# Attention heads of an AdaLN block: a one-piece row gather, key loads with another dimension outermost, and inverse roots in Newton steps

## The chip, the cores and the metric

The kernel runs on one core of a Trainium2 chip. Its time is the device time in microseconds (us), as the median of several runs. The core has a matrix engine (TensorE, PE in the profile), a vector engine (VectorE, DVE), a scalar engine (ScalarE, ACT), a general engine (GpSimd, POOL), and a queue engine (SyncE, SP) that here only starts transfers. They run in parallel and wait for each other through semaphores.

## The reference

x is (2, 2048, 256): two batches of 2048 tokens. Each batch goes through an attention layer that computes only the rows it selects, and then through a soft mixture of experts.

```
h = layernorm(x) * (1 + ca) + sa
q, k, v = heads of h @ Wq + bq, h @ Wk + bk, h @ Wv + bv      # 16 heads of width 16
scores = q k^T / 4
top_idx = top_k(scores.max(-1) - scores.mean(-1), 307)        # 307 of 2048 queries in each head
out = zeros; out[top_idx] = softmax(q[top_idx] k^T / 4) v
x = x + ga * (out @ Wo + bo)
h = layernorm(x) * (1 + cb) + sb
xn = h / max(norm(h), 1e-12) * 16 * gamma                     # per token
logits = xn sn^T                                              # 8 experts x 128 slots
eo = experts(softmax over tokens); y = softmax over slots of logits, times eo
x = x + gb * y
```

## The kernel before, in words

Tokens lie in 16 tiles of 128. For each batch in turn there are a search (score maxima of all 16 heads), a selection (a rank for each query in each head), and the attention over the selected queries, here "the head loop". The expert layers of both batches come after that: logits of 16 tiles, 8 experts, and a mix of 16 tiles. Queries and keys are kept in DRAM as three bfloat16 parts, whose products, six of them for each of the 16 dimensions (96 rows), restore float32 precision.

The head loop is the stage that the change touches most. The order on each engine is written out by hand. For head n, PE does this (`pe_head`, with line numbers of the kernel before):

- `scores` (L1960), in pairs k = 0 to 7, two products each: keys of 2 x 128 tokens against the 307 selected queries. ScalarE takes each pair out of PSUM with an exponential (`exps`, L905). The pairs use two PSUM places in turn, so pair k waits for the exponential of pair k-2. Pairs 0 and 1 of head n+1 are done inside head n, after its pair 7.
- `values` (L1969): 2 x 8 tiles of values times exponentials. The first half stands behind pair 5. The second half stands behind pairs 0 and 1 of the next head, and waits for all eight exponentials of its own head.
- `gather` (L1941): 16 products of a one-hot matrix, one for each token tile, which pick the 307 query rows. VectorE builds the one-hot matrix (`onehot`, L1414). The result goes to ScalarE (`take_gathered`, L893), then PE copies its parts to the 96 rows (`spread`, L1948, with a constant matrix `spread_rows`), and ScalarE takes that (`take_queries`, L898) as the queries of the next head. Gather and spread use one PSUM bank.
- `rows` (L1977) and `turn` (L1984): the row numbers of the selected queries, and the transposition of the finished output of the head before. VectorE divides (`finish`). In batch 1, GpSimd then scatters the rows to DRAM with three indirect transfers for each head (L726). In batch 0 those scatters are put off to the search of batch 1.

SP loads the 96 key rows (4 KB each) of a head in three transfers, of 48, 32 and 16 rows (`head_keys`, L487). There are two key buffers, so the transfers of head n+2 start when pair 7 of head n is through, and pair 0 of head n+2 waits for them. In `k_parts` the 48 rows are 3 parts x 16 dimensions.

The other part of the change is the square roots. In batch 1's head loop the second layer norm and the row norms of batch 0 are made on the side: variances in `spread`, a ScalarE square root (`root`, L946), a correction on VectorE (`refine`, L1102 to L1110), the normalised tile (`second_norm`, L1318 and L1322), its square on ScalarE (`square`, L952), another root for `rms`, and `xn_tile` (L1337), which gives the expert stage its input. The square root and the exponential live in different tables of ScalarE. For batch 1 the same is done at the start of, and inside, the mix of batch 0's experts (L2165 transpositions, L2175 products, L1027 and L1020 on ScalarE).

Of the kernel before, what the change touches and what calls it, by code (L numbers as in the profile page):

```python
# [17 lines left out]
I32 = mybir.dt.int32  # L18
# [6 lines left out]
LN_EPS = 1e-5  # L25
# [50 lines left out]
def adaln_block(nc, x, Wq, bq, Wk, bk, Wv, bv, Wo, bo, gamma, slot_gamma, slot_embeds,  # L76
# [60 lines left out]
    with ExitStack() as ctx:  # L137
# [241 lines left out]
        def _(sp):  # L379
# [102 lines left out]
            def head_keys(b, i, par):  # L482
# [124 lines left out]
        def _(pool):  # L607
# [31 lines left out]
            for half in range(2):  # L639
                for at, part in enumerate((0, 0, 0, 1, 1, 2)):  # L640
                    cols = spread_rows[:, at * DH:(at + 1) * DH]
                    g.affine_select(out=cols, in_=cols, compare_op=ALU.not_equal, fill=1.0, base=-(half * HALF_ROWS + part * DH), pattern=[[-1, DH]], channel_multiplier=1)
# [159 lines left out]
        def _(act):  # L802
# [85 lines left out]
            def attend(b):  # L888
# [53 lines left out]

            def root(n):

                act.wait_ge(var_ready, n)
                s.activation(rs_y[:], rs_v[:], ACT.Sqrt).then_inc(sqrt_done, 1)  # L946
# [7 lines left out]
            def experts(b):  # L954
# [78 lines left out]
                if b == 0:  # L1033
                    root(7)
                    for t in range(NT - 2):
# [4 lines left out]
                        if t == NT // 2:  # L1040
                            root(8)
                else:
                    with act.Fori(0, NT // 2 - 1) as i:
                        for par in range(2):
                            combine_turned(i, par)
                            combine_exp(i, par, par + 2)
# [48 lines left out]
        def _(dve):  # L1095
# [16 lines left out]


# [186 lines left out]
            def spread(b):  # L1300
# [7 lines left out]
                v.tensor_scalar(rs_v[:], mv[:, :, 1], LN_EPS, None, ALU.add).then_inc(var_ready, 1)  # L1308

            def spread_roots(b):  # L1310

                dve.wait_ge(sqrt_done, 4 + 3 * b)
                refine(NT, rstd[:], 1.0)
# [11 lines left out]
            def row_spread(b, at, end):  # L1325

                dve.wait_ge(ss_ready, 1 + NT * b + end)
                v.tensor_scalar(rs_v[:, at:end], ss[:, at:end], NORM_MIN * NORM_MIN, None, ALU.max).then_inc(var_ready, 1)

            def row_roots(n, at, end):  # L1330

                dve.wait_ge(sqrt_done, n)
                refine(end, rms[:, at:end], RMS, at)
# [72 lines left out]
            def attend(b):  # L1406
# [847 lines left out]
```

## Time and profile before

| | |
|---|---|
| time, median of 3 runs | 1620.09 us (1619.43 to 1622.69) |
| the profiled execution, its own time | 1618.59 us |
| its span in the profile | 1616.8 us |
| PE busy | 1475.0 us (91%) |
| DVE busy | 1201.0 us (74%) |
| ACT busy | 1052.9 us (65%) |
| score products of the head loop, L1960 and L905 | 512 PE products, 256 exponentials |

The profile is of one execution. Its span leaves out 1.8 us of that execution's time. Busy PE time counts overlapping ends, so a PE that is 91% busy still has gaps that matter. What sets the end is read from the chain of waits and from the order in time on each engine. The head loops lie at about 450 to 575 us (batch 0) and 938 to 1071 us (batch 1).

### The profile page before, as it was taken

To read this page: it belongs to the slowest core of one execution; us is meant where nothing else is said; L and a number is where in the kernel's file an instruction comes from. 1 tells how busy PE (TensorE), PEld (TensorE's weight loads), DVE (VectorE), ACT (ScalarE), POOL (GpSimd) and SP (SyncE) were. 2 spreads that over 40 slices of the span, in tenths; PEclk is the share of its full clock that TensorE was granted. 3 is DMA by queue.
4 is the path that set the end of the run, shared out by engine and by line. 5 is a ranking of instruction groups with operands and counts; after the bars stand their busy time and mean duration, and the time that the engine had idled before them with its cause. 6 is when DMAs were issued, how large, how long until landed. Compare 5 with 4: busy or idle time off the path is not lost.

```text
span 1616.8 us, 28401 instructions
## 1 busy us (share of the span) xinstructions
PE 1475.0 (91%) x8701; PEld 806.6 (50%) x8706; DVE 1201.0 (74%) x2750; ACT 1052.9 (65%) x1436; POOL 271.3 (17%) x334
## 2 busy tenths in 40 slices
PE   7999999998889989999998888979999999989999
PEld 3532222223434422222223634434899886489988
DVE  6679999999876669999999877756765443675511
ACT  4578888887677778888886557753433572334464
POOL 2440000003510051111111213330111000011100
PEclk9999999999999999999999989999999999999999
DMA  5861111121522201111212211120144202014410
GB/s 173 258 164 39 39 49 49 39 86 46 163 80 70 66 21 44 40 41 40 52 51 70 78 31 52 52 81 0 40 160 147 89 33 71 0 54 142 161 49 32
DMA packets 93458, 119.39 MB, mean 74 GB/s; under 512 B 22862, under 2 KB 78766, under 8 KB 92860
## 3 DMA queue, kind: packets, MB, share of 16 engines
q1 hardware_dynamic: 90300, 117.66, 23.8%
q0 software_dynamic: 3072, 0.66, 0.3%
q8 instruction: 44, 0.72, 0.2%
q14 instruction: 42, 0.34, 0.1%
HBM read 93.46 MB, written 24.79 MB: 73 GB/s over the span
## 4 chain that ended last, share of the span: by engine, by line
PE 46%; DVE 32%; issue 13%; ACT 4%; DMA 3%; POOL 1%; SPq 0%; DVEq 0%; another core or an unknown queue 0%; ACTq 0%; PEld 0%; PEldq 0%; POOLq 0%
DVE work_area L1282 25%; PE psum L2111 7%; PE psum L2175 6%; PE psum L1969 4%; PE psum L1960 4%; PE psum L2054 4%; PE psum L2122 3%; DVE big_area L1282 2%; PE psum L2131 2%; PE psum L1941 2%; DMA work_area<-heads_out 2%; PE psum L1769 2%; PE psum L2165 2%; PE psum L1794 1%; ACT big_area L962 1%
## 5 line engine op out<-in xcount | busy, mean ns | idle before, releaser
L1282 DVE CUSTOM_DVE_ANT_0 work_area<-psum,work_area 128x1024 f32<-128x1024 f32 x512 | 589.1, 1220 | 8.0 <-PE psum L1830 4.3
L883 ACT ACTIVATE work_area<-psum 128x1024 f32<-128x1024 f32 x512 | 510.4, 1027 | 74.5 <-DVE big_area L1282 30.7
L1830 PE MATMUL psum<-work_area 96*128 96x512 bf16 x1024 | 309.2, 384 | 47.9 <-DVE big_area L1282 6.8
L1820 PE MATMUL psum<-work_area 96*128 96x512 bf16 x1024 | 305.4, 380 | 7.4 <-ACT work_area L883 1.7
L1830 PEld LDWEIGHTS psum<-work_area 96*128 96x128 bf16 x1024 | 63.4, 97 | 266.3 <-DVE big_area L1282 243.5
L1820 PEld LDWEIGHTS psum<-work_area 96*128 96x128 bf16 x1024 | 88.8, 98 | 153.0 <-ACT work_area L883 58.3
L905 ACT ACTIVATE work_area<-psum 128x614 f32<-128x614 f32 x160 | 102.3, 682 | 39.0 <-PE psum L1960 38.4
L2111 PE MATMUL psum<-work_area,xn 128*128 128x128 f32 x1024 | 117.7, 276 | 0.0
L2175 PE MATMUL psum<-expert_out,work_area 128*128 128x256 f32 x512 | 115.6, 379 | 1.1 <-ACT work_area L1027 1.1
L2054 PE MATMUL psum<-slots_T,work_area 128*128 128x512 f32 x256 | 116.5, 599 | 0.0
L2111 PEld LDWEIGHTS psum<-work_area,xn 128*128 128x128 f32 x1024 | 116.3, 193 | 0.2
L1414 DVE TENSOR_SCALAR big_area<-iota,rank 128x308 bf16<-128x308 f16 x512 | 113.8, 300 | 0.1
L1960 PE MATMUL psum<-work_area 99*128 99x307 bf16 x512 | 94.4, 303 | 20.0 <-issue 6.6
L2175 PEld LDWEIGHTS psum<-expert_out,work_area 128*128 128x128 f32 x512 | 95.1, 190 | 13.1 <-ACT work_area L1027 1.3
L962 ACT ACTIVATE big_area<-psum 128x1024 f32 (+1 forms) x32 | 32.8, 1024 | 88.5 <-PE psum L2054 88.5
L1619 DVE SCALAR_TENSOR_TENSOR work_area<-psum,rz,x_res 128x256 f32<-128x256 f32 x32 | 15.5, 484 | 100.0 <-PE psum L2175 65.5
L741 POOL DMA_INDIRECT heads_out<-Wqk_sb x48 | 48.7, 1015 | 213.8 <-DVE big_area L1282 213.0
L1504 DVE TENSOR_TENSOR work_area<-work_area,big_area 128x1024 f32<-128x1024 f32 x32 | 39.2, 1226 | 49.1 <-ACT big_area L962 49.1
L757 POOL TENSOR_TENSOR work_area<-big_area,work_area 128x1024 f32 (+1 forms) x16 | 38.6, 2415 | 196.8 <-PE psum L2115 172.6
L1960 PEld LDWEIGHTS psum<-work_area 99*128 99x128 bf16 x512 | 39.9, 100 | 62.2 <-ACT work_area L905 20.2
L2054 PEld LDWEIGHTS psum<-slots_T,work_area 128*128 128x128 f32 x256 | 46.8, 193 | 47.6 <-issue 47.2
L905 ACT ACTIVATE expert_out<-psum 128x614 f32<-128x614 f32 x96 | 62.5, 680 | 9.8 <-PE psum L1960 8.2
(262 smaller groups left out, 2085.4 us busy)
## 6 DMA issues: line engine op xcount, KB each, us to landing
work_area<-in_L_ffn_w_dram SPq DMA_DIRECT2D x32, 1024.0 KB, 5.2
work_area<-k_parts SPq DMA_DIRECT2D x192, 64.2 KB
work_area<-q_parts SPq DMA_DIRECT2D x192, 64.0 KB
k_parts<-work_area SPq DMA_DIRECT2D x24, 384.0 KB, 3.5
q_parts<-work_area SPq DMA_DIRECT2D x16, 384.0 KB, 3.1
big_area<-q_parts SPq DMA_DIRECT2D x16, 384.0 KB, 5.9
work_area<-k_parts SPq DMA_DIRECT2D x32, 192.0 KB
x_res<-in_L_attn_x_dram SPq DMA_DIRECT2D x8, 512.0 KB, 6.4
```

What stands on the lines that cost most here:

```text
L883: s.activation(SC[:, t % 4], PS[:, 2 * (n % 2):2 * (n % 2) + 2].rearrange("p a n -> p (a n)"), ACT.Relu).then_inc(relu_done, 1)
L905: s.activation(PX[k][:, :, 0:U], PS[:, 2 * (k % 2):2 * (k % 2) + 2, 0:U], ACT.Exp, scale=SCALE).then_inc(p_ready, 1)
L962: s.activation(row(LS, i * 2 + par), PS[:, 2 + 2 * par:4 + 2 * par].rearrange("p a n -> p (a n)"), ACT.Identity).then_inc(lg_copied, 1)
L1282: v.tensor_tensor_reduce(SC[:, t % 4], PS[:, 4 + 2 * (t % 2):6 + 2 * (t % 2)].rearrange("p a n -> p (a n)"), SC[:, t % 4], 1.0, -3.0e38, A ...
L1414: last = v.tensor_scalar(OH[:, par, t], iota[:], rank[:, t, bass.ds(h, 1)], None, ALU.is_equal)
L1820: last = mm(PS[:, 2 * (n % 2) + k], QS1[par][0:TERMS, t * P:(t + 1) * P], KS[par][0:TERMS, k * 512:(k + 1) * 512], start=True, stop=True)
L1830: last = mm(PS[:, 4 + 2 * (t % 2) + k], QS1[par][0:TERMS, t * P:(t + 1) * P], KS[par][0:TERMS, K1 + k * 512:K1 + (k + 1) * 512], start=Tru ...
L1960: last = mm(PS[:, 2 * (k % 2) + kk, 0:U], K2S[n % 2][0:TERMS + 3, kt * P:(kt + 1) * P], QS[0:TERMS + 3, n % 2, 0:U], start=True, stop=True)
L1969: last = mm(PS[at:at + DH + 1, 6 - n % 2, 0:U], V[:, kt, i * 2 + n], PX[kt // 2][:, kt % 2, 0:U], start=(kt < 4), stop=(kt >= NT - 4), ski ...
L2054: last = mm(PS[:, 2 + 2 * par + k], XT[:, par, cc], SNT[:, cc, k * 512:(k + 1) * 512], start=(cc == 0), stop=(cc == DC - 1))
L2111: last = mm(PS[:, cc, 0:P], XN[:, t, cc * P:(cc + 1) * P], E1[:, t], start=(t == 0), stop=(t == NT - 1))
L2175: last = mm(PS[:, 5 - par, 0:D], E2T[:, par, e], EO[:, e], start=(e == 0), stop=(e == E - 1))
```

## The change

There are three edits.

1. `pe_head`: head n+1's gather is done whole (16 products) behind pairs 2 and 3 of head n. Before, tiles 8 to 15 stood there, and tiles 0 to 7 of head n+2's gather stood behind pairs 6 and 7.
2. `head_keys`: the DRAM side of each key transfer is given with the dimension ahead of the part, so its outermost size is 16 and not 3, 2 or 1. Each transfer still moves the same rows. Since the rows arrive in another order, `spread_rows` is filled to match.
3. The inverse roots of the second layer norm and of the row norms come from `inverse_roots` on VectorE: a first guess from the bits and three Newton steps, ten small instructions. `root` is gone from ScalarE. `spread_roots` moves from behind head 2 to behind head 1. The row norms of tiles 0 to 7 stand behind head 13, and the first two `xn_tile` behind head 14. The mix loop of the last batch on ScalarE is written out.

```diff
-                    sp.dma_start(K2S[par][at:at + n * DH, :], k_parts[b][0:n, bass.ds(h0, DH), K1:KW]).then_inc(k2_in[par], 16)
+                    sp.dma_start(K2S[par][at:at + n * DH, :], k_parts[b][0:n, bass.ds(h0, DH), K1:KW].rearrange("r p n -> p r n")).then_inc(k2_in[par], 16)
...
                 for h in range(H):
                     act_head(h // 2, h % 2, h < H - 1)
                     if b == 1:
-                        if h == 1:
-                            root(4)
                         if h < H - 1:
                             for t in tiles_of_head(h - 1):
                                 square(0, t)
                 if b == 1:
-                    root(5)
                     for t in range(NT - 4, NT):
                         square(0, t)
-                    root(6)
...
+            def inverse_roots(out_, at, end):
+
+                v_, y_, a_ = rs_v[:, at:end], rs_y[:, at:end], rs_a[:, at:end]
+                v.tensor_scalar(y_.bitcast(I32), v_.bitcast(I32), -0.5, float(0x5F3759DF), ALU.mult, ALU.add).then_inc(vstep, 1)
+                dve.wait_ge(vstep, vs.next())
+                for k in range(3):
+                    v.tensor_tensor(a_, y_, y_, ALU.mult).then_inc(vstep, 1)
+                    dve.wait_ge(vstep, vs.next())
+                    v.scalar_tensor_tensor(out=a_, in0=a_, scalar=-0.5, in1=v_, op0=ALU.mult, op1=ALU.mult).then_inc(vstep, 1)
+                    dve.wait_ge(vstep, vs.next())
+                    v.scalar_tensor_tensor(out=out_ if k == 2 else y_, in0=a_, scalar=1.5, in1=y_, op0=ALU.add, op1=ALU.mult).then_inc(vstep, 1)
+                    dve.wait_ge(vstep, vs.next())
...
-                        if h == 2:
-                            spread_roots(0)
-                        if h == H - 1:
-                            row_spread(0, 0, NT - 4)
+                        if h == 1:
+                            spread_roots()
+                        if h == H - 3:
+                            row_norms(0, 0, NT // 2)
+                        if h == H - 2:
+                            for par in range(2):
+                                xn_tile(0, par, par)
                         second_norm(0, tiles_of_head(h))
                     finish(PAIRS - 1, 1, 1)
-                    row_roots(5, 0, NT - 4)
-                    for par in range(2):
-                        xn_tile(0, par, par)
-                    row_spread(0, NT - 4, NT)
-                    row_roots(6, NT - 4, NT)
+                    row_norms(0, NT // 2, NT)
...
                     if later > 0 and not first:
-                        gather(i, n + 1, range(0 if second else NT // 2, NT))
+                        gather(i, n + 1, range(NT))
...
-                    if later > 1 and not first:
-                        gather(i, n + 2, range(NT // 2))
                     if not first:
                         turn(i, n - 1)
```

The first place is on PE, one head of the loop, from the spread for the next head to pairs 4 and 5 of the next head. `work_area` and `expert_out` hold queries, keys and exponentials, `big_area` the one-hot matrix or the values. Before:

```order
L1948 MATMUL psum<-work_area,spread_rows 101x307
L1960 MATMUL psum<-work_area 128x307 x4
L1941 MATMUL psum<-big_area,work_area 64x307 x8
L1984 MATMUL psum<-identF,work_area 128x128 x3
L1960 MATMUL psum<-work_area 128x307 x4
L1969 MATMUL psum<-expert_out,big_area 17x307 x4
L1969 MATMUL psum<-work_area,big_area 17x307 x4
L1960 MATMUL psum<-work_area 128x307 x4
L1941 MATMUL psum<-big_area,work_area 64x307 x8
L1977 MATMUL psum<-idx_rows,work_area 128x1 x2
L1977 MATMUL psum<-idx_rows,work_area 51x1
L1960 MATMUL psum<-work_area 128x307 x4
```

The same place on PE after the change, where the lines of these functions have moved up by three:

```order
L1945 MATMUL psum<-work_area,spread_rows 101x307
L1957 MATMUL psum<-work_area 128x307 x4
L1981 MATMUL psum<-identF,work_area 128x128 x3
L1957 MATMUL psum<-work_area 128x307 x4
L1966 MATMUL psum<-expert_out,big_area 17x307 x4
L1966 MATMUL psum<-work_area,big_area 17x307 x4
L1957 MATMUL psum<-work_area 128x307 x4
L1938 MATMUL psum<-big_area,work_area 64x307 x16
L1974 MATMUL psum<-idx_rows,work_area 128x1 x2
L1974 MATMUL psum<-idx_rows,work_area 51x1
L1957 MATMUL psum<-work_area 128x307 x4
```

Eight gather products went from between pairs 6, 7 and the transposition to behind pairs 2, 3. Between pairs 6, 7 and the next pairs 0, 1 only the three transpositions are left.

The second place is on DVE, at the start of the mix of batch 0's experts: the last rows before the first `second_norm` of batch 1 (`mean_var` is the variances, `rstd` the inverse roots). Before:

```order
L1305 BN_AGGR mean_var<-stat 128x2 x16
L1308 TENSOR_SCALAR rs_v<-mean_var 128x16
L1555 TENSOR_TENSOR work_area<-psum,work_area 128x256
L1557 TENSOR_TENSOR expert_out<-work_area,mod_rows_sb 128x256
L1102 RECIPROCAL rs_a<-rs_y 128x16
L1104 TENSOR_TENSOR rs_a<-rs_a,rs_v 128x16
L1106 TENSOR_TENSOR rs_a<-rs_a,rs_y 128x16
L1108 RECIPROCAL rs_a<-rs_a 128x16
L1110 TENSOR_SCALAR rstd<-rs_a 128x16
L1318 SCALAR_TENSOR_TENSOR xn<-x_res,mean_var,mod_rows_sb 128x256 x2
```

After the change, on DVE, from the same expert output to the same step:

```order
L1555 TENSOR_TENSOR expert_out<-work_area,mod_rows_sb 128x256
L1313 TENSOR_SCALAR rs_v<-mean_var 128x16
L1106 TENSOR_SCALAR rs_y<-rs_v 128x16
L1109 TENSOR_TENSOR rs_a<-rs_y 128x16
L1111 SCALAR_TENSOR_TENSOR rs_a<-rs_a,rs_v 128x16
L1113 SCALAR_TENSOR_TENSOR rs_y<-rs_a,rs_y 128x16
L1109 TENSOR_TENSOR rs_a<-rs_y 128x16
L1111 SCALAR_TENSOR_TENSOR rs_a<-rs_a,rs_v 128x16
L1113 SCALAR_TENSOR_TENSOR rs_y<-rs_a,rs_y 128x16
L1109 TENSOR_TENSOR rs_a<-rs_y 128x16
L1111 SCALAR_TENSOR_TENSOR rs_a<-rs_a,rs_v 128x16
L1113 SCALAR_TENSOR_TENSOR rstd<-rs_a,rs_y 128x16
```

Between the expert output and the first `second_norm` there stood five small instructions, and now there are eleven.

The third place is on ACT, at the end of batch 1's head loop. Before, the last exponentials are followed by a table load and two roots:

```order
L905 ACTIVATE work_area<-psum 128x2x307 x2
L946 ACT_TABLE_LOAD
L946 ACTIVATE rs_y<-rs_v 128x16
L952 ACTIVATE work_area,sumsq<-xn 128x256 x4
L946 ACTIVATE rs_y<-rs_v 128x16
L958 ACTIVATE work_area<-psum 128x256
```

After the change, on ACT, L958 has become L951:

```order
L907 ACTIVATE work_area<-psum 128x2x307 x3
L907 ACTIVATE expert_out<-psum 128x2x307 x3
L907 ACTIVATE work_area<-psum 128x2x307 x2
L945 ACTIVATE work_area,sumsq<-xn 128x256 x4
L951 ACTIVATE work_area<-psum 128x256
```

Both roots and the table load are gone, and the four squares lead straight to the first copy of the expert stage.

## Rows read from the trace of the kernel before

**Rows 1.** PE in time, one head of batch 0; us start, us length, [idle before].

```profile
528.80 0.69 PE L1960 MATMUL psum<-work_area 99*128 99x307 bf16 x4
529.58 0.71 PE L1941 MATMUL psum<-big_area,work_area 128*64 128x307 bf16 x8
530.22 0.55 PE L1984 MATMUL psum<-identF,work_area 128*128 128x128 f32 x3
531.33 0.68 PE L1960 MATMUL psum<-work_area 99*128 99x307 bf16 x4 [0.56 <-issue]
531.94 0.71 PE L1969 MATMUL psum<-expert_out,big_area 128*17 128x307 f32 x8
533.11 0.70 PE L1960 MATMUL psum<-work_area 99*128 99x307 bf16 x4
536.59 0.69 PE L1960 MATMUL psum<-work_area 99*128 99x307 bf16 x4
```

**Rows 2.** SP in time, the key transfers issued two heads earlier.

```profile
522.10 1.88 SPq L487 DMA_DIRECT2D work_area<-k_parts  x3
```

**Rows 3.** ACT in time, in that head.

```profile
529.33 1.25 ACT L905 ACTIVATE work_area<-psum 128x614 f32<-128x614 f32 x2
531.79 1.26 ACT L905 ACTIVATE work_area<-psum 128x614 f32<-128x614 f32 x2 [1.21 <-PE psum L1960]
```

**Rows 4.** The chain of waits in the last heads of batch 0.

```profile
562.08 7.15 DMA work_area<-k_parts
```

**Rows 5.** Stretches: busy time (count) by engine, PE clock, DMA share, GB/s.

```profile
562.00:569.00 7.00, 5.65 (x60) 2.67 (x59) 1.89 (x8) 5.45 (x10) 0.00 (x0) 1.00 0.21 57
570.10:573.50 3.40, 3.30 (x23) 1.24 (x16) 0.48 (x1) 1.68 (x4) 0.00 (x0) 0.50 0.02 5
```

**Rows 6.** The page's DMA issues: count, KB each, us from issue to landing.

```profile
k_parts<-work_area SPq DMA_DIRECT2D x24, 384.0 KB, 3.5
big_area<-q_parts SPq DMA_DIRECT2D x16, 384.0 KB, 5.9
```

**Rows 7.** PE in time: a whole gather, first and last spread of 13 periods, last head.

```profile
464.73 1.24 PE L1941 MATMUL psum<-big_area,work_area 128*64 128x307 bf16 x16
467.94 0.34 PE L1948 MATMUL psum<-work_area,spread_rows 128*101 128x307 bf16 x1
566.46 0.34 PE L1948 MATMUL psum<-work_area,spread_rows 128*101 128x307 bf16 x1
569.94 0.63 PE L1969 MATMUL psum<-expert_out,big_area 128*17 128x307 f32 x4
```

**Rows 8.** PE in time, batch 1: the wait in head 2, and spreads of 12 periods.

```profile
959.43 1.01 PE L1960 MATMUL psum<-work_area 99*128 99x307 bf16 x4 [1.70 <-ACT work_area L905]
963.05 0.34 PE L1948 MATMUL psum<-work_area,spread_rows 128*101 128x307 bf16 x1
1010.79 0.34 PE L1948 MATMUL psum<-work_area,spread_rows 128*101 128x307 bf16 x1
1059.26 0.34 PE L1948 MATMUL psum<-work_area,spread_rows 128*101 128x307 bf16 x1
```

**Rows 9.** POOL in time, the third scatter of one head of batch 1.

```profile
1010.14 1.07 POOL L726 DMA_INDIRECT heads_out<-work_area  x1 [0.30 <-issue]
```

**Rows 10.** ACT in time, that head, and the end of batch 1's head loop.

```profile
1012.02 0.43 ACT L898 ACTIVATE work_area<-psum 101x307 bf16<-101x307 f32 x1 [0.93 <-PE psum L1948]
...
1073.16 0.19 ACT L952 ACTIVATION_READ_ACCUMULATOR work_area<-xn 128x1 f32 x1
1075.38 0.37 ACT L958 ACTIVATE work_area<-psum 128x256 f32<-128x256 f32 x1
```

**Rows 11.** DVE in time, the third tile's input, and a small step of `refine`.

```profile
1078.24 0.48 DVE L1337 SCALAR_TENSOR_TENSOR work_area<-xn,rms,gamma_row 128x256 f32<-128x256 f32 x1 [1.75 <-POOL xn L751]
...
1284.99 0.17 DVE L1106 TENSOR_TENSOR rs_a<-rs_a,rs_y 128x16 f32<-128x16 f32 x1
```

**Rows 12.** PE in time, the second tile of the first mix.

```profile
1289.08 3.29 PE L2175 MATMUL psum<-expert_out,work_area 128*128 128x256 f32 x14 [1.09 <-ACT work_area L1027]
```

More of the change, by code:

```diff
@@ L639, in _ @@
             for half in range(2):
-                for at, part in enumerate((0, 0, 0, 1, 1, 2)):
-                    cols = spread_rows[:, at * DH:(at + 1) * DH]
-                    g.affine_select(out=cols, in_=cols, compare_op=ALU.not_equal, fill=1.0, base=-(half * HALF_ROWS + part * DH), pattern=[[-1, DH]], channel_multiplier=1)
+                at = 0
+                for part, n in enumerate((3, 2, 1)):
+                    cols = spread_rows[:, at:at + n * DH].rearrange("p (d r) -> p d r", r=n)
+                    g.affine_select(out=cols, in_=cols, compare_op=ALU.not_equal, fill=1.0, base=-(half * HALF_ROWS + part * DH), pattern=[[-1, DH], [0, n]], channel_multiplier=1)
+                    at += n * DH
                 cols = spread_rows[:, TERMS:TERMS + 5]
@@ L941, in take_heads @@
                 s.activation(AT[:, t % 2], PS[:, turn_bank(b, t), turn_at(b, t):turn_at(b, t) + D], ACT.Identity).then_inc(at_ready, 1)
-            def root(n):
-                act.wait_ge(var_ready, n)
-                s.activation(rs_y[:], rs_v[:], ACT.Sqrt).then_inc(sqrt_done, 1)
             def square(b, t):
@@ L1033, in experts @@
                 if b == 0:
-                    root(7)
                     for t in range(NT - 2):
@@ L1039, in experts @@
                             square(1, k)
-                        if t == NT // 2:
-                            root(8)
-                else:
-                    with act.Fori(0, NT // 2 - 1) as i:
-                        for par in range(2):
-                            combine_turned(i, par)
-                            combine_exp(i, par, par + 2)
+                else:
+                    for t in range(NT - 2):
+                        combine_turned(t // 2, t % 2)
+                        combine_exp(t // 2, t % 2, t % 2 + 2)
                 for par in range(2):
@@ L1307, in spread, with spread_roots @@
                 dve.wait_ge(vstep, vs.next())
[L1308 to L1313, printed above, removed]
+            def spread_roots():
+                v.tensor_scalar(rs_v[:], mv[:, :, 1], LN_EPS, None, ALU.add).then_inc(vstep, 1)
+                dve.wait_ge(vstep, vs.next())
+                inverse_roots(rstd[:], 0, NT)
             def second_norm(b, tiles):
@@ L1323, in second_norm, with row_norms @@
                                            op0=ALU.mult, op1=ALU.add).then_inc(h2_ready, 1)
-            def row_spread(b, at, end):
+            def row_norms(b, at, end):
                 dve.wait_ge(ss_ready, 1 + NT * b + end)
[L1328 to L1333, printed above, removed]
+                v.tensor_scalar(rs_v[:, at:end], ss[:, at:end], NORM_MIN * NORM_MIN, 1.0 / D, ALU.max, ALU.mult).then_inc(vstep, 1)
+                dve.wait_ge(vstep, vs.next())
+                inverse_roots(rms[:, at:end], at, end)
             def xn_tile(i, par, n):
@@ L1594, in experts @@
                     expert_out(E - 1, 0, vs.next())
-                    spread_roots(1)
+                    spread_roots()
                 else:
@@ L1627, in experts @@
                             v.memset(CM, -3.0e38).then_inc(cmax_done, 1)
-                            row_spread(1, 0, NT)
-                            row_roots(8, 0, NT)
+                            row_norms(1, 0, NT)
                         if t >= NT - 2:
```

1 line of the change is left out of this document (removed).

## The prediction

> **What bounds the kernel now.** I read the chain of waits first, to see which stages carry the end; then PE, ACT and SP in order of time inside one head of the loop; then stretches of time, for the transfers and PE's clock; last the page's table of transfers. In the head loop PE is the bound, with one gap in each head: 0.56 us ahead of pairs 0 and 1 of the next head [rows 1]. The view can't name its releaser ("issue"). I read it as the key transfers. Those for the pair at 531.33 were started at 522.10 [rows 2], so if they end the gap they take 9.2 us from first issue to landing. Where the chain does name them, in the last head of batch 0, it shows 7.15 us of DMA behind the last issue at 562.08, till 569.23 [rows 4]. With the 1.88 us that the three issues take, that is 9.0 us, the same length. In that stretch 0.21 of the 16 DMA engines is busy, at 57 GB/s [rows 5]: a head's keys (96 rows of 4 KB, 393 KB) need 6.9 us at that rate. So few engines do the work, and it is their time that each head waits for.
>
> Call T the start of pairs 6 and 7 of a head. T is 528.80, and the next is 536.59: a period of 7.79. Over 13 periods of batch 0 it is (566.46 - 467.94) / 13 = 7.58 [rows 7]. The loop closes on the keys: they start at T + 1.1 (522.10, where T was 528.80 - 7.79 = 521.01), and land 9.1 later, which must be before pair 0 of two heads on.
>
> **The change part by part.**
>
> *The key transfers.* The nearest rows for another shape are transfers of the same 384 KB on 128 rows: 3.5 us from issue to landing for a write, 5.9 for a load [rows 6]. With 1.9 of issues the new length is between 1.9 + 3.5 = 5.4 and, if nothing changes, 9.1. I take 5.4 to 6, since the load of 5.9 is of short runs and this is of 4 KB rows. The wait is then not late in any head: pair 0 comes at T + period + 1.3, so the transfers have 7.5 us. What is late next is ScalarE, below.
>
> The Trainium skill ("DMA: Bandwidth & Descriptors", section on why a DMA increments its semaphore by 16 and not by 1) says that such a transfer is split over k engines, k being the largest number up to 16 that divides the outermost size of both sides. By it, the three transfers ran on 3, 2 and 16 engines, and now run on 16 each. The trace agrees with the first half: a share of 0.21 is 3.4 engines [rows 5]. No row shows the second half. By the rule the time on the busiest engine falls from 33 rows of 4 KB to 6; by the rows alone it may not fall at all, and that is the rival that ends slower.
>
> *The gather.* Products neither come nor go, eight of them move. They were the work that PE had between pairs 6, 7 and the next pairs 0, 1, and that covered ScalarE: exponentials 6 and 7 run from 529.33 to 530.58, that is to T + 1.78 [rows 3]. Before, PE reached the next pair 0 at T + 2.53 with the wait, and at about T + 1.8 without. Now only the transposition stands between, so PE is there at about T + 1.0 and waits: pair 0 for exponential 6, pair 1 for exponential 7. Its signal arrives 0.06 after the end (533.05 to 533.11) [rows 1, 3], so pair 1 starts at T + 1.84, takes 0.31 (half of 531.33 to 531.94), and the value products start at T + 2.17, where they started at T + 3.14. From there to the next T it was 536.59 - 531.94 = 4.65. Eight more gather products stand in it now: a whole gather takes 1.24 and a half 0.71, so 0.53 more [rows 1, 7]. New period: 2.17 + 4.65 + 0.53 = 7.35. So of the gap that the transfers leave, some is handed back as a wait on ScalarE. With the old order the period without the gap would be 7.79 - 0.56 = 7.23 or less: the move alone costs some 0.1 to 0.3 a head. Behind the gather, `take_gathered` on ScalarE comes 0.53 later; exponential 4 waits for pair 4, which is 0.53 later itself, so this costs nothing. On VectorE the one-hot of a head is ready half a head earlier than it is needed.
>
> Batch 0: 98.5 - 13 x 7.35 = 2.9 us. Its last head: the value products stood at 569.94, and come at 566.46 + 0.17 + 2.17 = 568.80, so 1.1. Behind the long wait PE ran at half clock (1.2 GHz; granted 0.50) from 570.10 for 3.4 us, and did in it what takes 1.7 at the full 2.4 GHz [rows 5]. Without a long wait ahead of it I don't expect the fall, and take 1.2 of the 1.7, as ScalarE bounds a head with no gather (0 to 1.7).
>
> Batch 1: 12 periods take 1059.26 - 963.05 = 96.2, so 8.02 each [rows 8]. Here the signals of PE's products come late around GpSimd's scatters: the spread starts at 1010.79, and ScalarE gets it 1.23 later, idle for 0.93, while GpSimd runs an indirect transfer from 1010.14 to 1011.21 [rows 8 to 10]. That delay stands in the period before (gather and pair 0 wait behind it). Whether it stays exposed depends on where the scatters fall in the new order. They start after `finish`, which follows the transposition. That stands some 0.3 earlier against the value products, and the pairs 4, 5 and the spread stand 0.53 later, so by my count they fall mostly outside. The ends are 7.35 (no delay) and 7.92 (one exponential of 0.57 late in each head). I take 7.5: 96.2 - 90 = 6.2 (1.2 to 8.0). The last head of batch 1 gains 1.1 as that of batch 0.
>
> *The roots.* Removed from ScalarE in head 2: PE waited 1.70 there behind two table loads [rows 8]. On VectorE the eleven small instructions of about 0.21 each (0.17 [rows 11] and an estimate of 0.04 between them) take 2.3 us behind head 1, where VectorE waits over 2 us a head; that is 1.7 gained. The row norms behind head 13 lie where no one-hot is built any more, and are hidden too. At the end of the loop the first expert tiles are ready before, so the first copy of the expert stage starts when ScalarE has done its squares: at 1073.35 where it was 1075.38 [rows 10], 2.0, and 0.1 for a small instruction gone ahead of them. The third tile isn't late by this: its input came at 1078.24 behind GpSimd's copy [rows 11], and the first tile's logits hold PE till then anyway. At the mix the chain is the other way: VectorE now does eleven instructions instead of five between the expert output and `second_norm` (one of the six more had been hidden), ScalarE's square and copy wait for it, and PE already waited 1.09 for that copy [rows 12]. So 6 x 0.21 = 1.2 less what the removed table loads give ScalarE: I take a loss of 1.1 (0 to 1.3). The roots inside the mix are hidden before and after; so are the table loads in the last mix, where PE has work for a whole tile.
>
> The sum: 2.9 + 1.1 + 1.2 + 6.2 + 1.1 + 1.7 + 2.1 - 1.1 = 15.2 us off the profiled execution's 1618.6, which gives 1603.4. That execution lies 1.5 below the median of the runs, so the forecast for the median is 1605.
>
> **The rivals.**
>
> *A. The scatters' delay stays in every head of batch 1.* For it: it stood in nearly every head before, and the moved gather's own signal may now fall into it. Against it: by count the exponentials 6 and 7 start clear of it. Then 7.92 in batch 1, 1.2 instead of 6.2: 5 us less, 1610.
>
> *B. The transfers stay as slow.* This ends slower, as the filler is gone and the wait isn't. With a length of 9.1 and a start at T + 1.1, pair 0 must stand at T + 10.2, and it comes at T + period + 1.26. With g as the gap, 7.35 + g + 1.26 + g = 10.2 gives g = 0.8 and a period of 8.15. Batch 0 loses 13 x 0.57 = 7.4, batch 1 some 12 x 0.2 = 2.4, and the rest gives 1.2 + 1.7 + 2.1 - 1.1 = 3.9: 5.9 slower, 1626. It decides from a length of about 8 us (7.35 + g = 7.58, g = 0.23) on. Against it: the same kilobytes on 128 rows land in 3.5 to 5.9.
>
> *C. More than the count.* The delays in batch 1 vanish, the clock's fall at the head of the expert stage too (PE is idle there for 2 us less), and the heads run at 7.25. Then 13 x 0.1 + 12 x 0.25 = 4.3 from the periods, and some 1.5 from the clock on top: 1599.
>
> *D. Almost nothing.* The move of the gather costs what the transfers give (a period of 7.6 in batch 0, 8.0 in batch 1), and only the ends stay: 1.1 + 1.2 + 1.1 + 1.7 + 2.1 - 1.1, 6 us: 1614.
>
> **How the numbers follow.** My forecast 0.52, A 0.18, C 0.16, D 0.08, B 0.06. The range for 8 in 10 is 1598 to 1612.5, from C to past A. A measurement of this kernel tells 0.2% (3.2 us) from no change. Faster by more than that are the forecast, A, C and most of D: 0.91. Same: 0.04, from D and B. Slower: 0.05, B.
>
> **What would show it.** Period of the spread, batch 0, at 7.3 to 7.4, with PE's two short waits now ahead of pairs 0 and 1 and released by the exponentials; 7.06 to 7.2 would show that ScalarE isn't late, 7.6 and more that the gather's move or the transfers cost. The key transfers landing within 6 us of their first issue, spread over more engines. No wait for keys in the last heads, and no half clock at 570. In batch 1 a period of 7.5. No table load in head 2. The first expert copy right behind the squares, and a longer wait of PE for its second tile at the first mix. The forecast is wrong if the key transfers are late again, or if batch 1's heads stay at 8.

## The result, and where the time went

The changed kernel takes 1617.67 us (median of 18 runs, 1614.1 to 1621.43), the kernel before 1620.32 beside it (18 runs, 1616.37 to 1625.61). The ratio is 0.9983, 95% interval 0.9976 to 0.999: by 0.2%, no change that counts. 1605.0 was forecast, within 1598 to 1612.5. The forecast was wrong.

The profiled execution has a span of 1619.5 us (own time 1621.43), so it is on the slow side of its runs by 3.8, and 2.7 above the span shown of before. The page of after:

```profile
span 1619.5 us, 28340 instructions
PE 1481.0 (91%) x8701; PEld 810.5 (50%) x8706; DVE 1204.9 (74%) x2775; ACT 1033.8 (64%) x1418; POOL 271.0 (17%) x328
```

**Batch 0 came as forecast.** PE in one head of batch 0, after (start, duration, line, products; the last bracket is PE's wait and its releaser). It answers to [rows 1]:

```profile
519.97 0.69 PE L1957 MATMUL psum<-work_area 99*128 99x307 bf16 x4
520.49 0.49 PE L1981 MATMUL psum<-identF,work_area 128*128 128x128 f32 x3
521.31 0.92 PE L1957 MATMUL psum<-work_area 99*128 99x307 bf16 x4 [0.33 <-ACT work_area L907]
522.16 0.71 PE L1966 MATMUL psum<-expert_out,big_area 128*17 128x307 f32 x8
523.95 1.24 PE L1938 MATMUL psum<-big_area,work_area 128*64 128x307 bf16 x16
527.33 0.69 PE L1957 MATMUL psum<-work_area 99*128 99x307 bf16 x4
```

T is 519.97, the next 527.33: a period of 7.36. The wait ahead of pair 0 has a name now, exponential 6 on ScalarE, and the value products start at T + 2.19 (2.17 forecast). The keys are early:

```profile
520.78 1.83 SPq L487 DMA_DIRECT2D work_area<-k_parts  x3
```

By the trace's semaphore records the last piece of these three transfers landed at 524.87, 4.1 us after the first issue. For the transfers issued at 522.10 before [rows 2], it was 531.24, so 9.1 us, 0.09 before pair 0 at 531.33 [rows 1].

**Batch 1 did not.** The spreads of batch 1 in after, and those of batch 0 (first and last start of a line's instructions):

```profile
L1945 PE MATMUL psum<-work_area,spread_rows x13: 335/335/335, 958.5 to 1062.0; 128*101 128x307 bf16 x13
L1945 PE MATMUL psum<-work_area,spread_rows x14: 335/335/335, 468.2 to 564.0; 128*101 128x307 bf16 x14
```

12 periods take 103.5 us, 8.62 each, where before took 96.2 [rows 8] and 90 was forecast. What waited, after, 958 to 1062 us (who, for what: us in total, times, longest):

```profile
ACT work_area L895 <- remote: 20.9, 10, 2.4
PE psum L1945 <- ACT work_area L895: 4.1, 10, 0.7
PE psum L1957 <- ACT work_area L907: 2.8, 12, 0.3
PE psum L1957 <- ACT expert_out L907: 2.4, 10, 0.2
```

L895 is `take_gathered`, which waits for the gather's last product and waited 0.6 us in all in the same stretch of before. In the head at 1023 us that product ends at about 1024.7 by the timeline, its increment (the signal) is recorded at 1026.64, and `take_gathered` starts at 1026.66. The signals of `rows` and of pairs 4 and 5, whose products end between 1025.0 and 1025.6, are recorded from 1026.69 to 1026.78. The last of the head's three scatters ran from 1024.97 to 1026.06. Behind `take_gathered`, ScalarE's queue holds exponentials 4 and 5, `take_queries` and exponentials 6 and 7. Exponential 4 starts at 1026.99; it couldn't have started before 1026.73 in any case, as its own signal was late too.

PE's clock fell besides. It was at 1.2 GHz three times inside these 12 periods (at 969.9, 1004.0 and 1055.2 us, 3.4 us each), and never inside those of before. One of the three, with the stretches around it (PE, PEld, DVE, ACT, POOL busy, granted clock, DMA share, GB/s):

```profile
961.00:969.90 8.90, 7.54 (x73) 3.48 (x73) 6.48 (x29) 5.75 (x13) 3.08 (x3) 1.00 0.20 49
969.90:973.30 3.40, 3.40 (x22) 0.93 (x20) 0.50 (x3) 1.41 (x5) 1.96 (x3) 0.50 0.41 118
973.30:977.00 3.70, 3.70 (x43) 1.95 (x42) 3.67 (x17) 2.78 (x5) 1.06 (x1) 1.00 0.04 6
```

The three periods with a fall are 9.5, and the one behind it is 7.8. The first of the 12 is 8.69, and the six others are 8.43 in the mean. So the late signals make 8.43 of 7.36. The three falls add 0.4, 0.5 and 1.1 us (each with the shorter period behind it, which the last doesn't have in the count).

### The profile page after: what moved, and what is told of

It reads as the page before. It is cut to its first block, busy times and chain, and to the rows that moved or that the text cites. A ratio compares the mean times of both kernels' runs of the same rounds, so it can differ in the third digit from the quotient of the medians.

```text
span 1619.5 us, 28340 instructions
## 1 busy us (share of the span) xinstructions
PE 1481.0 (91%) x8701; PEld 810.5 (50%) x8706; DVE 1204.9 (74%) x2775; ACT 1033.8 (64%) x1418; POOL 271.0 (17%) x328
## 4 chain that ended last, share of the span: by engine, by line
PE 45%; DVE 32%; issue 13%; ACT 6%; DMA 3%; POOL 1%; SPq 0%; DVEq 0%; ACTq 0%
DVE work_area L1284 25%; PE psum L2106 7%; PE psum L2170 6%; PE psum L1966 5%; PE psum L2049 4%; PE psum L1957 4%; PE psum L2117 3%; DVE big_area L1284 2%; PE psum L1938 2%; PE psum L2126 2%; ACT work_area L907 2%; PE psum L1766 2%; DMA work_area<-heads_out 2%; PE psum L2160 2%; PE psum L1791 1%
## 5 line engine op out<-in xcount | busy, mean ns | idle before, releaser
L1957 PE MATMUL psum<-work_area 99*128 99x307 bf16 x512 | 100.4, 306 | 19.2 <-ACT work_area L907 10.1
L728 POOL DMA_INDIRECT heads_out<-work_area x48 | 50.2, 1046 | 102.8 <-DVE work_area L1441 91.3
```

Source lines behind the costliest of these rows:

```text
L728: g.indirect_dma_start(out=heads_out[b], out_offset=bass.IndirectOffsetOnAxis(ap=IDX[0:w, par, j:j + 1], axis=0), in_=ON[0:w, par, j], in_ ...
L1957: last = mm(PS[:, 2 * (k % 2) + kk, 0:U], K2S[n % 2][0:TERMS + 3, kt * P:(kt + 1) * P], QS[0:TERMS + 3, n % 2, 0:U], start=True, stop=True)
```

## The experiments

The runs came to six chips or more, and these are of two kinds. I call them by their trace: on chips with **late signals** increments of PE's semaphores are recorded up to 2.2 us after the product beside scatters, and ScalarE starts only then; on the **others** none is late. Periods are from one profile each; b0 is 13 periods of batch 0, b1 the last 12 of batch 1; the last column is the ratio to the kernel before on the same chip.

| kernel | chip | b0 | b1 | median us | before | ratio (95%) |
|---|---|---|---|---|---|---|
| before (first profile) | late | 7.58 | 8.02 | 1620.32 | | |
| after | late | 7.36 | 8.62 | 1617.67 | 1620.32 | 0.9983 (0.9976-0.999) |
| keys_only | late | 7.06 | 7.78 | 1606.43 | 1618.99 | 0.9921 (0.9903-0.994) |
| gather_only | late | 8.02 | 8.50 | 1628.10 | 1618.99 | 1.0046 (1.0029-1.0063) |
| roots_only | late | 7.64 | 7.98 | 1617.48 | 1618.99 | 0.9994 (0.9978-1.0009) |
| keys_roots | late | 7.06 | 7.92 | 1603.76 | 1618.99 | 0.9901 (0.9883-0.9919) |
| halves_in_b1 | other | 7.36 | 7.15 | 1599.49 | 1613.17 | 0.9915 (0.9895-0.9935) |
| deferred_one | other | 7.36 | 7.36 | 1620.00 | 1613.17 | 1.0035 (1.0019-1.0051) |
| deferred | other | 7.06 | 7.13 | 1613.11 | 1613.17 | 0.9998 (0.9982-1.0014) |
| copies_on_act | other | 7.06 | 7.15 | 1593.44 | 1613.17 | 0.9883 (0.9863-0.9904) |
| after_again | other | 7.36 | 7.36 | 1602.70 | 1614.92 | 0.9925 (0.9905-0.9944) |
| before_again | other | 7.69 | 7.94 | 1614.05 | 1614.92 | 0.9989 (0.9975-1.0003) |
| keys_roots_again | other | 7.06 | 7.15 | 1595.99 | 1614.92 | 0.9881 (0.986-0.9901) |
| no_scatter | other | 7.36 | 7.36 | 1601.35 | 1614.92 | 0.9922 (0.9902-0.9942) |
| after_third | other | 7.36 | 7.36 | 1600.84 | 1616.05 | 0.9907 (0.9875-0.9939) |
| no_scatter_third | other | 7.36 | 7.36 | 1601.86 | 1616.05 | 0.9910 (0.988-0.994) |
| copies_on_act_third | other | 7.06 | 7.15 | 1592.84 | 1616.05 | 0.9856 (0.9824-0.9888) |
| half_scatters | other | 7.36 | 7.36 | 1600.91 | 1613.93 | 0.9914 (0.988-0.9948) |
| half_scatters_2 | late | 7.36 | 7.36, then 8.43 | 1610.06 | 1621.20 | 0.9928 (0.990-0.9956) |

### One part of the change at a time

keys_only is the kernel before with this edit (and `spread_rows` filled to match):

```diff
-  k_parts[b][0:n, bass.ds(h0, DH), K1:KW]).then_inc(k2_in[par], 16)
+  k_parts[b][0:n, bass.ds(h0, DH), K1:KW].rearrange("r p n -> p r n")).then_inc(k2_in[par], 16)
```

> The kernel before with the key transfers in the new order of rows, nothing else of the change. Theory S (GpSimd's scatters hold back TensorE's signals, and the gather in one piece puts its own signal in that window): without the moved gather batch 1 keeps the period of before or a little less, 7.8 to 8.0 us; batch 0 loses the wait for keys: 7.1 to 7.25 instead of 7.58, so 13 x 0.4 = 5 off; no 7 us wait in the last head. In all 6 to 8 us faster (ratio 0.995 to 0.9965), more than the whole change. Rival T (the new transfers themselves disturb batch 1, by more engines at once): a period of 8.4 in batch 1 as with the whole change, and no gain in all. Rival U (ScalarE bounds the heads in any order): 7.36 in batch 0 here too.

gather_only is the kernel before with `gather(i, n + 1, range(NT))` behind pairs 2 and 3 and without the half behind pairs 6 and 7.

> The kernel before with the gather in one piece behind the second score pair, nothing else. Theory S: batch 1 at 8.4 us a head (8.02 before), 12 x 0.4 = 5 more, with take_gathered on ScalarE waiting some 2 us in each head; batch 0 at about 8.1 since the keys still take 9 us and the filler ahead of pair 0 is gone: 13 x 0.5 = 6.5 more. In all 9 to 13 us slower (ratio 1.006 to 1.008). Rival T (the transfers disturb batch 1, the gather doesn't): batch 1 stays at 8.0 to 8.2, in all 6 to 8 slower.

roots_only has `inverse_roots` and its places, and nothing else. keys_roots is the changed kernel with the gather as before:

```diff
-                        gather(i, n + 1, range(NT))
+                        gather(i, n + 1, range(0 if second else NT // 2, NT))
...
+                    if later > 1 and not first:
+                        gather(i, n + 2, range(NT // 2))
```

> The kernel before with the roots by Newton steps on VectorE, nothing else. Theory S: batch 1's third head 1.4 us shorter, the other heads at 8.02 as before; what the end of the loop gains is mostly given back behind GpSimd's copy of the third tile, and the first mix loses about 1: in all 1 to 3 us faster (ratio 0.998 to 0.9995). Rival V (VectorE's new work is what lengthens batch 1's heads): a period of 8.4 in batch 1 and 2 to 4 us slower in all.

> The changed kernel with the gather in two halves as before: all of the change but the moved gather. Theory S: batch 0 at 7.1 to 7.25, batch 1 at 7.8 to 8.0, the third head without table loads: 8 to 10 us faster than before (ratio 0.994 to 0.995), and so faster than the whole change by 6. Rivals T and V (transfers or roots lengthen batch 1): batch 1 at 8.4 also here and no faster than the whole change (ratio 0.998).

The keys alone give 12.6 us, most of the gain and more than I had expected (6 to 8): 6.7 in batch 0, 2.9 in batch 1's 12 periods. With the roots it is 15.2, where 8 to 10 was expected. The roots alone give 1.5, which the noise doesn't tell from nothing. The gather alone loses 7.5 by the ratio (9 to 13 expected); its profile has the clock at half for 3.4 us in one head of each batch, which took 10.05 and 10.29. So one edit of the three works against the change: keys_roots is 13 us (by the ratios) faster than the whole change on the same kind of chip. T, U and V fall: in keys_only batch 1 is at 7.78 and batch 0 at 7.06, in gather_only batch 1 is at 8.50, and in roots_only at 7.98.

### The gather in one piece, and the scatters

halves_in_b1 keeps the piece in batch 0 and has the two halves in batch 1.

> The changed kernel with the gather of batch 1 in two halves as before; in batch 0 it stays in one piece. Theory S (the piece costs 0.3 us a head by ScalarE's wait in batch 0, and 0.7 to 0.8 in batch 1 where its signal falls into GpSimd's scatters): batch 0 at 7.36, batch 1 at 7.8 to 8.0, in all 1608 to 1610. Rival W (what the piece costs in batch 1 is the same 0.3 as in batch 0, and the rest was the clock, which fell three times in that profile): 1613 to 1614, with batch 1 at 8.1 to 8.2 where no half clock stands.

It ran at 7.06 in all of batch 1's last 11 heads (the mean of 7.15 holds one of 8.11), with the scatters in place: neither S nor W allowed that. The same code in batch 1 had taken 7.92 in keys_roots. The chip was the difference, and the next three runs, all on one chip, ask that question.

> The changed kernel once more, beside the kernel before and two others on one chip, since the runs so far came from two chips whose traces differ: on one, batch 1's heads take 7.8 to 7.9 with halves, TensorE's signals 0.5 to 2.4 us late beside the scatters; on the other the same order takes 7.06 and no signal is late. Theory Y (whether the scatters hold back signals is a property of the chip or of the run, and only where they do does the moved gather cost 11 us in batch 1): where signals are late, a period of 8.4 to 8.6 and 1617 to 1620; where they aren't, 7.36 in both batches, 1602 to 1606 with the kernel before at 1613. Rival Z (the gather in one piece is what brings the late signals, on any chip): 8.4 to 8.6 on either chip.

> The kernel before once more, for its profile on this chip. Theory Y: where signals are late, 7.58 and 8.02 a head in the two batches as in the first profile; where they aren't, 7.5 in both, some 6 us less in all. Its ratio to itself is 1.

> The changed kernel with the gather in two halves. Theory Y: 7.06 in batch 0 on any chip; in batch 1 7.8 to 7.9 where signals are late and 7.06 to 7.15 where they aren't; 1603 or 1594 to 1596. In both cases faster than the whole change: by 13 to 15 us where signals are late, by 26 x 0.3 = 8 where not.

Y holds and Z falls. In after_again the changed kernel has 7.36 in each head of both batches; 13 spreads of batch 1:

```profile
L1945 PE MATMUL psum<-work_area,spread_rows x13: 335/335/335, 953.8 to 1042.2; 128*101 128x307 bf16 x13
```

No signal is late in it, and `take_gathered` waits 2.1 us in all 12 heads where it had waited 20.9 in ten (958 to 1062 us):

```profile
PE psum L1957 <- ACT work_area L907: 4.3, 13, 0.4
ACT work_area L895 <- PE psum L1938: 2.1, 12, 0.2
```

There the change is worth 12.2 and, in after_third, 15.2 us (15.2 forecast). The kernel before is faster on such a chip too, by some 3 to 8 us in the medians, though batch 1 is at 7.94 for 8.02 in the profile. That mean holds one head of 11.92, in which PE waited 1.9 us for the keys and then ran at half clock for 6.8; the eleven others take 7.57. Its keys are late on either kind.

Whether the scatters are the cause can only be seen on a chip with late signals. no_scatter leaves out batch 1's scatters, and ran on two of the others.

> The changed kernel without the scatters of batch 1 (its heads' outputs are computed but not written, so this work is left out). Theory S: where signals are late with the scatters, this kernel's batch 1 has a period of 7.36, that of batch 0, and no late signal: 13 x 1.2 = 14 to 16 less than the changed kernel beside it. Where they aren't late, 7.36 in both and no difference in the heads. Rival W (something else in batch 1's heads): 8 or more stays without the scatters.

> The changed kernel as the reference of this chip. If signals are late here: 8.4 a head in batch 1 where TensorE's clock doesn't fall, 1617 to 1620. If not: 7.36 and 1601 to 1605.

> The changed kernel without the scatters of batch 1 (left out: its heads' outputs are not written). If the scatters hold the signals back: 7.36 a head on any chip, and on one with late signals 13 to 16 us less than the changed kernel. Rival (such a chip delays signals whatever GpSimd does): 8.4 here too.

Where no signal is late, leaving the scatters out changes nothing: 7.36 and 7.36, 1601.35 beside 1602.7, 1601.86 beside 1600.84. The next kernel carries its own control, heads 0 to 7 of batch 1 without scatters and 8 to 15 with:

```diff
-                with pool.Fori(0, PAIRS) as i:
+                with pool.Fori(PAIRS // 2, PAIRS) as i:
                     for par in range(2):
                         scatter(i, par)
```

> The changed kernel, with the scatters of batch 1's heads 0 to 7 left out (those heads are not written) and those of heads 8 to 15 kept. If the scatters hold the signals back, on a chip with late signals: heads 0 to 7 at 7.36, and 8.4 and late signals from head 9 on. If such a chip delays signals by itself: 8.4 in all heads. On a chip without late signals: 7.36 throughout, which decides nothing.

> The changed kernel, with the scatters of batch 1's heads 0 to 7 left out (those heads are not written) and those of heads 8 to 15 kept, once more. If the scatters hold the signals back, on a chip with late signals: heads 0 to 7 at 7.36, and 8.4 and late signals from head 9 on. If such a chip delays signals by itself: 8.4 in all heads. On a chip without late signals: 7.36 throughout, which decides nothing.

half_scatters ran on a chip without late signals (7.36 throughout), half_scatters_2 on one with. Its spreads from 962 to 1001 us, without scatters, and from 1020 to 1050, with them:

```profile
L1945 PE MATMUL psum<-work_area,spread_rows x6: 335/335/335, 963.9 to 1000.7; 128*101 128x307 bf16 x6
L1945 PE MATMUL psum<-work_area,spread_rows x4: 334/335/335, 1024.3 to 1049.6; 128*101 128x307 bf16 x4
```

(1000.7 - 963.9) / 5 = 7.36 and (1049.6 - 1024.3) / 3 = 8.43, in one execution and at full clock. The gather and `take_gathered` in one head of each kind, PE and ScalarE of half_scatters_2, first without scatters:

```profile
997.48 1.24 PE L1938 MATMUL psum<-big_area,work_area 128*64 128x307 bf16 x16
...
1000.69 0.34 PE L1945 MATMUL psum<-work_area,spread_rows 128*101 128x307 bf16 x1
...
998.76 0.43 ACT L895 ACTIVATE work_area<-psum 128x307 bf16<-128x307 f32 x1 [0.18 <-PE psum L1938]
999.37 1.25 ACT L907 ACTIVATE expert_out<-psum 128x614 f32<-128x614 f32 x2 [0.18 <-PE psum L1957]
```

and with them (PE, ScalarE, GpSimd):

```profile
1020.61 1.24 PE L1938 MATMUL psum<-big_area,work_area 128*64 128x307 bf16 x16
...
1024.29 0.34 PE L1945 MATMUL psum<-work_area,spread_rows 128*101 128x307 bf16 x1 [0.41 <-ACT work_area L895]
...
1023.81 0.43 ACT L895 ACTIVATE work_area<-psum 128x307 bf16<-128x307 f32 x1 [2.10 <-remote]
1024.13 1.25 ACT L907 ACTIVATE expert_out<-psum 128x614 f32<-128x614 f32 x2
...
1019.41 0.98 POOL L728 DMA_INDIRECT heads_out<-work_area  x1 [4.61 <-DVE work_area L1441]
1020.70 1.12 POOL L728 DMA_INDIRECT heads_out<-work_area  x1 [0.30 <-issue]
1022.12 1.11 POOL L728 DMA_INDIRECT heads_out<-work_area  x1 [0.30 <-issue]
```

From the gather's start to `take_gathered` it is 1.28 us without scatters and 3.20 with. In this one execution the gather's signal is 0.02 us late in all of the heads without scatters from 954 to 1007 us, and 1.91 to 1.96 in the five with them. The scatters are the cause, on the chips where there are late signals. Whether the products' results land late or only their signals, the trace doesn't tell. In halves (keys_roots) the window hits another signal: the half gather's is on time (0.02 in the last ten heads) and `take_gathered` doesn't wait, but the spread's is late, by 0.74 to 1.06 in twelve heads. This costs 7.92 against 7.15, or 0.77 a head, where the piece pays 1.07.

### The scatters out of the heads

deferred keeps all heads' outputs of batch 1 (as batch 0 does), scatters them during batch 0's logits, and moves GpSimd's copies there to ScalarE; deferred_one has the gather in one piece besides. The core of it:

```diff
+            def scatter_in_logits():
+                pool.wait_ge(on_ready, B * H)
+                for h in range(H):
+                    for j in range(CH):
+                        w = min(P, U - j * P)
+                        g.indirect_dma_start(
+                            out=heads_out[1], out_offset=bass.IndirectOffsetOnAxis(ap=IDX0[0:w, h, j:j + 1], axis=0),
+                            in_=ON0[0:w, h, j], in_offset=None).then_inc(scattered[h % 2], 16)
```

> The changed kernel (gather in one piece) with the scatters of batch 1 moved out of the heads: VectorE keeps all heads' outputs and indices, as in batch 0, GpSimd scatters them while the logits are made, and ScalarE makes the copies that GpSimd made there. Theory S: batch 1's period falls to that of batch 0, 7.36, with no wait of take_gathered on ScalarE beyond 0.3; 13 x 1.1 = 14 us off the changed kernel, 1601 to 1604, if the scatters disturb the logits little. Rival W (the clock, or the work that only batch 1's heads have: the norms on VectorE, the squares on ScalarE): a period of 8 or more stays.

> The changed kernel with the gather in two halves as before and the scatters of batch 1 moved out of the heads as in deferred_one. Theory S: 7.06 in both batches; 12 x 0.85 = 10 us less than with halves and scatters in the heads (1603.8), so 1592 to 1595, and 1590 if the third tile of the expert stage was held up by GpSimd's copy. Rival X (the delay only moves: 48 scatters in 65 us hold back the signals of the logits, or the first transfers of the heads' rows come late): 1600 or more.

X holds: deferred is 17 us behind keys_roots on a like chip (1613.1, 1596.0), where it was expected ahead, and deferred_one 17 to 19 behind after. The chain of waits of deferred (start, duration) and the two rows of PE after it:

```profile
1121.15 0.99 POOL heads_out L753
1122.44 0.96 POOL heads_out L753
1123.71 2.30 DMA heads_out<-Wqk_sb
1126.47 2.44 DMA work_area<-heads_out
```

```profile
1107.83 3.17 PE L2065 MATMUL psum<-slots_T,work_area 128*128 128x512 f32 x7
1128.21 1.43 PE L1868 MATMUL psum<-identF,work_area 128*128 128x128 f32 x4 [17.22 <-issue]
```

GpSimd starts the last of the 48 scatters at 1123.7, it lands 2.3 us later, and the heads' rows can be loaded only then. PE waits 17.2 us, and its clock is at half from 1114.8 for 17.1 us. Neither version ran on a chip with late signals, where the saving in the heads would stand against this; that stays open.

### A version that beats both

copies_on_act is keys_roots with `s.activation(row(XN, i * 2 + n), XS[:, par], ACT.Identity)` behind the copy of each turned tile, in place of GpSimd's copy (batch 0's expert stage alone).

> The changed kernel with the gather in two halves as before, and the copies of the normalised tiles in batch 0's logits on ScalarE instead of GpSimd; the scatters stay in the heads. If the third tile of the expert stage is held up by GpSimd, which still has the last heads' scatters ahead of its copy (theory: that is where the 2.1 us forecast for the start of the expert stage went), the second logits start 1.5 to 2.5 us earlier against the last take_out, and the time is 1602 against 1603.8. If it isn't the copy, no change or some 0.3 a tile of ScalarE's work in the way: 1604.

> Halves, new key transfers, Newton roots, and the copies of the first expert stage on ScalarE. On a chip with late signals 7.8 to 7.9 a head in batch 1 and 1600 to 1603; on one without 7.06 to 7.15 and 1592 to 1595, faster than the changed kernel on either by 9 to 17.

It is the fastest on both chips it ran on: 1593.44 (1602 expected, but for a chip with late signals) and 1592.84, 8 us below the changed kernel beside it (1600.84). Whether it beats keys_roots isn't settled, as no chip ran both: ratios of 0.9883 and 0.9856 against 0.9881. In after the third tile had waited for GpSimd (2.75 us, and 2.76 in after_again), and in copies_on_act it doesn't (VectorE):

```profile
1080.29 0.48 DVE L1336 SCALAR_TENSOR_TENSOR work_area<-xn,rms,gamma_row 128x256 f32<-128x256 f32 x1 [2.75 <-POOL xn L753]
```

```profile
1052.92 0.48 DVE L1339 SCALAR_TENSOR_TENSOR work_area<-xn,rms,gamma_row 128x256 f32<-128x256 f32 x1 [0.47 <-DVE rms L1116]
```

## Why the prediction was wrong, step by step

Us gained (-) or lost by each stretch: as forecast, in the first profiled pair (late signals), and in the pair before_again, after_again (others). What is left of the spans' difference, 0.3 and -1.2, lies ahead of batch 0's third spread. No forecast term covers it.

| term | forecast | late | other |
|---|---|---|---|
| batch 0, 13 periods | -2.9 | -2.8 | -4.3 |
| last head of batch 0, clock, search, to batch 1's first spread | -2.3 | -0.5 | 0.0 |
| first three heads of batch 1 (the roots) | -1.7 | -1.6 | -1.9 |
| batch 1, 12 periods | -6.2 | **+7.3** | -6.9 |
| from the last spread to the end | -2.1 | 0.0 | -2.1 |

- **The failed step is batch 1's period.** "By my count they fall mostly outside", it said, and "I take 7.5", with 7.92 as the upper end, "one exponential of 0.57 late in each head". The runs showed 8.43 at full clock and 8.62 in the profile. The count was of the spread, pairs 4 and 5, and exponentials 6 and 7. It was right for the spread, whose signal was late by 0.2 to 0.9 in twelve heads of before and is 0.01 late in after. It was wrong for pairs 4 and 5 (1.4 and 1.2 us late in the head at 1023), and it left out the gather's last product, the one that the change itself moves: its 16 products end just as the second scatter does, and the signal is 1.9 us late. And the price is not one exponential. The window's whole remainder counts, and 1.07 of the 1.9 stays on the path. How much of that is owed to the gather's signal and how much to those of pairs 4 and 5, no run separates. Rival A named the gather's signal ("the moved gather's own signal may now fall into it") and priced the period at 7.92.
- Rival A stood at 1610 with a period of 7.92. At full clock it was 8.43: 12 x 0.51 = 6.1 more, 1616, and 2 from the clock's three falls make 1618, where 1617.67 was measured. That this closes is luck: the table has 1.8 and 2.1 more lost in two other stretches, and the profiled execution is 3.8 above the median.
- On chips without late signals the number came out: 7.36 in batch 1, ratios of 0.9925 and 0.9907, 12.2 and 15.2 us faster, medians of 1602.7 and 1600.84. For batch 1's term that is partly luck. The 8.02 it started from holds late signals, which such a chip hasn't; eleven of before_again's heads take 7.57, so 12 x 0.21 = 2.5 us are gained on them, and the rest of the 6.9 is its one head of 11.92.
- *The key transfers.* Right in mechanism, and shorter than the 5.4 to 6 taken: 4.1 us. The half of the rule from "DMA: Bandwidth & Descriptors" of the Trainium skill (section on why a DMA increments its semaphore by 16 and not by 1) that no row had shown is shown by this: the same bytes in the order whose outermost size is 16 take 4.1 instead of 9.1. The trace agrees in the packets too: beside the 96 of 4 KB there were 21 of 4 bytes for a head's three transfers before (3 + 2 + 16), and there are 48 in after (16 for each). B, which needed 8 us, is out.
- *The gather's price in batch 0.* "The move alone costs some 0.1 to 0.3 a head": 7.36 against 7.06 in keys_roots, so 0.30, the top of that. The sum used 7.35 and was right (its 1.84 and 0.31 make 2.15 and not 2.17, which changes nothing). What was missing is that the old order with the new transfers, measured at 7.06, is the faster kernel.
- *The last head and the clock.* The search starts 11.6 us behind the last spread, where it was 13.9: 2.3, as forecast. But the half clock didn't go. It came at 577.3 for 6.8 us, in the search, where it had been at 570.1 for 3.4 [rows 5], and in the first pair 1.8 of the 2.3 is lost there. after_again had no fall there, and no gain over before_again either, whose profile had neither a fall nor a long wait there (its search starts 11.6 behind the last spread as well).
- *The roots.* Head 2 as forecast (7.75 for 9.15; 7.36 on the other chip). In halves the head behind it takes 8.10 to 8.11 instead of 7.06 in four profiles on the other chips. There PE waits 1.13 for the one-hot matrix (halves_in_b1), which VectorE starts right behind the roots' last step at 954.01. So the work on VectorE isn't hidden in every order.
- *The expert stage.* The first logits start 3.1 us behind the last `take_out`, 5.5 before: 2.3 gained, 2.1 forecast. "The third tile isn't late by this" was wrong: it waits 2.75 for GpSimd, which is still at the last scatters; copies_on_act takes that away. In the first pair the whole stretch gained nothing all the same (0.0 in the table). Counted from the last spread, PE is 2.6 us ahead when it turns the third tile, 1.5 at the end of the experts, and 0.3 at the second tile of the mix. The 1.1 lost before the mix stays unexplained.
- *The first mix.* PE waits 2.25 for ScalarE's copy where it was 1.09 [rows 12], a loss of 1.2; 1.1 forecast:

```profile
1291.51 3.72 PE L2170 MATMUL psum<-expert_out,work_area 128*128 128x256 f32 x16 [2.25 <-ACT work_area L1020]
```

## What to carry to other kernels

When a moved piece of work signals another engine, place its own signal, and those of the work that it pushes back, against every disturbance in the period first. Price a hit by how long the signal is held, and not by one instruction of the engine that waits. Cut a change into its parts before it is judged: here "no change" was a gain of 15 us less a loss of 13. And a profile is of one chip: what delays signals there may not exist on the next.

## What the runs showed that I had not expected

- Whether PE's semaphore increments are held back beside GpSimd's indirect transfers depends on the chip. In three groups of runs (before at 1619 to 1621) PE's increments are up to 2.2 us late beside them; in the four others (before at 1613 to 1616) none is. Why these chips differ stays open.
- The increments that are late are let go together, within 0.15 us: four signals from 1026.64 to 1026.78. VectorE isn't seen to be held: beside the scatters of one head in half_scatters_2 (1046 to 1048 us) its small steps, each of which waits for the one before, went on every 0.2 us. Records of increments are missing there (one between 1046.3 and 1047.8, for seven steps), so a late record counts only where the waiting engine starts late as well.
- Three transfers of the same 96 rows of 4 KB take 9.1 us or 4.1, by the order in which their dimensions are written.
